# Router logits by column quarters, gate bias by a 128-row selector, and routed bookkeeping one block ahead, in a graph-attention and expert kernel

## The chip, the cores and the metric

The kernel runs on one core of a Trainium2 chip. The metric is the device time of one execution in microseconds (us), from the first to the last instruction with what lies around it. The engines are TensorE (PE in the profile, with PEld for its weight loads), VectorE (DVE), ScalarE (ACT), GpSimd (POOL) and SyncE (SP), which issues most of the DMAs. Each engine runs its instructions in order, and they wait for each other through semaphores.

## The reference

There are 16 batches of 512 tokens with 256 features, in float32. What is computed, cut to its core:

```python
h = layernorm(x)
q, k, v = h @ Wq.T, h @ Wk.T, h @ Wv.T            # 8 heads of 32
c = softmax(where(adj, q k / sqrt(32), -inf)) @ v
gate = sigmoid(concat([c, h]) @ Wg.T + bg)
x = x + gate * h + (1 - gate) * c
f = layernorm(x)                                   # 8192 tokens
w, idx = top_k(softmax(f @ router_w), 2)           # 8 experts, 2 each
x = x + sum_k w_k * (silu(f @ Wg[e]) * (f @ Wu[e])) @ Wd[e] + (silu(f @ Sg) * (f @ Su)) @ Sd
```

## The kernel before

The kernel has two phases with a barrier between them.

**Attention phase.** Its loop goes over batches, in software-pipelined passes. Each pass has 32 positions, here called slots: one slot for each tile of 128 queries of one head. In a slot TensorE makes a score matmul (L439, 96 rows by 512 keys), and the four transposes of an older slot's probabilities (L449). VectorE adds the mask and takes the maximum (L792), ScalarE takes the exponential (L568) and copies the transposed probabilities to SBUF (`pt`, L556). Every eighth slot, TensorE multiplies the probabilities with V (L470), in four column quarters: the weights are 32 columns wide, and each head's result lands in 32 of the 128 partitions.

The other work of a batch is cut into units, and the table `UNIT_AT` gives each a slot. L is the router's logits of two batches back, Q, K and V are the projections, C the transposes of the attention's result, R the ranks of tokens in their expert, Z the gate for a quarter of the tokens, P and X are transposes of the normalised inputs. A unit writes one of three PSUM banks, and another engine copies it out; TensorE waits until the unit three before has been copied (`g_free`). So a pass runs in this order: L0 in slots 0 and 1, Q1 in 2 and 3, K1 in 4 and 5, V0 and V1 in 6 to 9, C0, C1, R0 in 10 to 12, Z0 to Z3 in 14 to 17, P0, P1 in 18 and 19, Q0, K0 in 22 to 25, X0, X1 in 29 and 30.

Matmuls whose operands are split in a high and a low float32r part come in threes (L354 to L356). L0 is in plain float32 (L412): for each of four token tiles and two halves of the features, 128 columns of `z` are the weights, and the 8 columns of `router_w` stream. The profile shows each such matmul as two records. Z begins with the bias (L397): a matmul with 2 rows of ones and the 2 rows of `bg2`, the high and the low part of the bias, 256 columns wide.

ScalarE copies the logits to `lg` (L516), and `choose` on VectorE takes the two best from there, in slot 3.

**Expert phase.** After 16 shared blocks come 39 routed blocks of 512 or 256 tokens, each with the weights of one expert. For each block n, TensorE makes gate and up products for parts 0 and 1, turns (transposes, L1261) the tokens `xb` of block n+1, makes the down product of block n-1 and then parts 2 and 3. VectorE casts and splits the weights of block n+1 (L1392, L1407), and makes `take(n)` between the product of part 2 and that of part 3: it reads from `xb` the token numbers (`ix`) and weights (`wt`) of the block, which ScalarE and GpSimd use for the scaled copy (L1348) and the scatter-add (L1155). `xb`, `ix` and `wt` each have two buffers. SyncE, in one queue, loads the weights (`raw`) and then `xb` of block n+1; the buffer of `xb` is free when block n-1 has been turned and taken:

```python
if not before:
    sp.wait_ge(s_tk, (n - SH) * TK)
load_routed(n + 1, 1 - s)
```

Of the kernel before, what the change touches and what calls it, by code (L numbers as in the profile page):

```python
# [5 lines left out]
P = 128  # L6
# [15 lines left out]

UNIT_AT = {"L0": 0, "Q1": 2, "K1": 4, "V0": 6, "V1": 8, "C0": 10, "C1": 11, "R0": 12, "Z0": 14, "Z1": 15, "Z2": 16,
           "Z3": 17, "P0": 18, "P1": 19, "Q0": 22, "K0": 24, "X0": 29, "X1": 30}
HALVES = "LQKV"

# [8 lines left out]
def attention_phase(nc, sems, x, adj, wqkv, wgate, bg, router_w, xn_dram, x1_dram, xt2_dram, xg_dram,  # L35
# [20 lines left out]
    RING = 8  # L56
# [6 lines left out]
    with ctx:  # L63
# [44 lines left out]
        bg2 = sb("bg2", [P, D], F32R)  # L108
        ones2 = sb("ones2", [P, P], F32R)
        rw = sb("rw", [P, KF, E])  # L110
        ident_b = sb("ident_b", [P, P], BF16)
        below = sb("below", [P, P], BF16)
# [62 lines left out]
        s_lo = sem("s_lo")  # L175
        s_half = sem("s_half")


# [40 lines left out]
        def has(b, name, att, pre, post):  # L219

            kind = name[0]
            return (late(b) if kind in "RL" else att if kind == "V" or name in ("Q1", "K1") else
                    post if kind in "CZX" else pre)
# [8 lines left out]

        def bank(par, name):
            return G[ORDER.index(name) % 3]

# [113 lines left out]
        def _(pe):  # L349
# [13 lines left out]
            def do_unit(b, par, name, piece, end):  # L363
                B, A = b + 1, b - 1
                o = bank(par, name)
                k = int(name[1])
# [25 lines left out]
                elif name[0] == "Z":  # L392
                    if isinstance(b, int) and b == 1:
                        pe.wait_ge(s_set, 7)
                    pe.wait_ge(g_free, unit(b, "C1") + 1)
                    tok = slice(P * k, P * k + P)
                    pe.matmul(o[:, 0:D], ones2[0:2, :], bg2[0:2, :], start=True, stop=False)  # L397
                    for kf in range(KF):
                        split(o[:, 0:D], xt_h[s][:, kf, tok], xt_l[s][:, kf, tok],
                              wg_h[:, KF + kf, :], wg_l[:, KF + kf, :], False, False)  # L400
                    for kf in range(KF):
                        last = split(o[:, 0:D], ct_h[:, kf, tok], ct_l[:, kf, tok],
                                     wg_h[:, kf, :], wg_l[:, kf, :], False, kf == KF - 1)
                elif name[0] == "X":
                    pe.wait_ge(s_xn2, A * NT + NT)
                    last = turn(o, xn2, k)
                elif name[0] == "L":
                    pe.wait_ge(g_free, unit(b - 1, "X1") + 1)
                    zt = z[:, :, :].rearrange("p i d -> p (i d)")
                    for i in (2 * piece, 2 * piece + 1):  # L410
                        for kf in range(KF):
                            last = pe.matmul(o[:, E * i:E * i + E], zt[:, N * kf + P * i:N * kf + P * i + P],  # L412
                                             rw[:, kf, :], start=kf == 0, stop=kf == KF - 1)
                elif name[0] == "R":

# [70 lines left out]
        def _(act):  # L486
# [4 lines left out]
            def evacuate(b, par, name):  # L491
                B, A = b + 1, b - 1
                o = bank(par, name)
                k = int(name[1])
                act.wait_ge(g_full, unit(b, name) + 1)
                if name[0] in "ZL":
                    act.wait_ge(g_free, unit(b, name))
# [13 lines left out]
                elif name[0] == "C":  # L511

                    act.activation(ct_h[:, k, :], o[:, :], ACT.Copy).then_inc(g_hi, 1)
                elif name[0] == "L":
                    act.wait_ge(s_rt, (b - 2) * RT)
                    act.activation(lg[:, :, :], o[:, 0:NT * E].rearrange("p (i e) -> p i e", e=E),  # L516
                                   ACT.Copy).then_inc(g_free, 1)
# [70 lines left out]
        def _(dve):  # L588
            zf = z[:, :, :].rearrange("p i d -> p (i d)")
            df = diff[:, :, :].rearrange("p i d -> p (i d)")  # L590

            dve.memset(f32(ones2[:, :]), 1.0).then_inc(s_set, 1)

# [6 lines left out]
            def prepare():  # L600
# [8 lines left out]

                dve.tensor_copy(bgh[:, :], bgt[:, :]).then_inc(s_set, 1)  # L610
                dve.wait_ge(s_set, 5)
                dve.tensor_tensor(wg_l[:, :, :], x1[:, :, :], f32(wg_h[:, :, :]), ALU.subtract).then_inc(s_lo, 1)
# [3 lines left out]
                dve.wait_ge(s_lo, 5)  # L616
                dve.wait_ge(s_rt0, 4)
                dve.nop().then_inc(s_set, 2)

# [20 lines left out]
            def low(b, par, name):  # L640

                B, A = b + 1, b - 1
                o = bank(par, name)
                k = int(name[1])
# [67 lines left out]
            def choose(A):  # L712

                rt = A * RT
                dve.wait_ge(g_free, unit(A + 2, "L0") + 1)
                dve.wait_ge(s_rt, rt)
# [209 lines left out]
def ffn_phase(nc, sems, w_dram, xt2_dram, x1_dram, xg_dram, out, ident, msum, xn2, idx, s_scat, nb, region,  # L926
# [50 lines left out]
    with ctx:  # L977
# [73 lines left out]
        wb = sb("wb", [P, NT])  # L1051
        wt = [sb(f"wt{s}", [P, NT]) for s in range(2)]
        ix = [sb(f"ix{s}", [P, NT], U32) for s in range(2)]

# [56 lines left out]
        def _(pool):  # L1111
# [29 lines left out]
            def add(n, s, first):  # L1141
# [12 lines left out]
                for i in range(tiles(n)):  # L1154
                    pool.indirect_dma_start(  # L1155
                        out=out, out_offset=bass.IndirectOffsetOnAxis(ap=ix[s][:, i:i + 1], axis=0),
                        in_=yb[s][:, i, :], in_offset=None, compute_op=ALU.add).then_inc(s_acc, 16)
# [165 lines left out]
        def _(act):  # L1323
# [13 lines left out]
            def out_(n, s, first):  # L1337
# [6 lines left out]
                for j in range(2):  # L1344
                    act.wait_ge(y_full, n * 2 + j + 1)
                    for ii in range(tiles(n) // 2):
                        i = tiles(n) // 2 * j + ii
                        last = act.activation(yb[s][:, i, :], OB[j][:, D * ii:D * ii + D], ACT.Copy,  # L1348
                                              scale=wt[s][:, i:i + 1])
                    last.then_inc(s_y[j], 1)  # L1350
# [27 lines left out]
        def _(dve):  # L1378
# [60 lines left out]
            def take(n, s):  # L1439
# [4 lines left out]
                dve.wait_ge(s_xb[s], (n - s) * 8 + 16)  # L1444
                if n >= SH + 2:
                    dve.wait_ge(s_acc, acc(r - 1))
                if n > SH:
                    dve.wait_ge(s_tk, t0)
                dve.nop().then_inc(s_held_dve, 1)
                dve.tensor_copy(own[:, :], (hef if is_half(r) else tef)[:, c:c + 1]).then_inc(s_tk, 1)  # L1450
                dve.tensor_copy(ix[s][:, 0:tl], xb[s][:, 0:tl, WT]).then_inc(s_tk, 1)
                dve.wait_ge(s_tk, t0 + 2)
# [4 lines left out]
                dve.wait_ge(s_tk, t0 + 4)  # L1457
                dve.tensor_tensor(wt[s][:, 0:tl], wa[:, 0:tl], wb[:, 0:tl], ALU.add).then_inc(s_tk, 1)

# [113 lines left out]
            def body(n, s, shared, before, after):  # L1573
# [13 lines left out]
                if after is not None:  # L1587
                    low_x(n + 1, 1 - s, after)
                if after is False:
                    high_routed(n + 1, 1 - s, 2)  # L1590
                    low_routed(n + 1, 1 - s, 2)
                if before:
                    out_shared(n - 1, 1 - s)
                mul(n, s, 2)
                if not shared:
                    take(n, s)
                mul(n, s, 3)
# [76 lines left out]
```

## Time and profile before

| | before |
|---|---|
| median of 3 runs | 1965.34 us (1961.91 to 1969.79) |
| the profiled execution | 1960.68 us, of which the span is 1959.0 us |
| busy: TensorE, VectorE, ScalarE, GpSimd | 91%, 66%, 56%, 34% of the span |
| mean granted TensorE clock | 0.973 of full speed |
| score matmuls (attention phase) | 27.1 to 947.1 us |
| turns of routed blocks | 1269.3 to 1918.5 us |

Times inside the profile are counted from the first instruction. A matmul's duration overlaps with its neighbours', so what counts is the time from one start to the next. A clock of 1.00 stands for 2.4 GHz, one of 0.50 for 1.2 GHz.

### The profile page before, as it was taken

To read this page: it belongs to the slowest core of one execution; us is meant where nothing else is said; L and a number is where in the kernel's file an instruction comes from. 1 tells how busy PE (TensorE), PEld (TensorE's weight loads), DVE (VectorE), ACT (ScalarE), POOL (GpSimd) and SP (SyncE) were. 2 spreads that over 40 slices of the span, in tenths; PEclk is the share of its full clock that TensorE was granted. 3 is DMA by queue.
4 is the path that set the end of the run, shared out by engine and by line. 5 is a ranking of instruction groups with operands and counts; after the bars stand their busy time and mean duration, and the time that the engine had idled before them with its cause. 6 is when DMAs were issued, how large, how long until landed. Compare 5 with 4: busy or idle time off the path is not lost. (4 is left out here: it accounts for less than half of the span.)

```text
span 1959.0 us, 36000 instructions
## 1 busy us (share of the span) xinstructions
PE 1791.2 (91%) x12597; PEld 1502.0 (77%) x12597; DVE 1293.2 (66%) x3149; ACT 1098.3 (56%) x2489; POOL 667.4 (34%) x515
## 2 busy tenths in 40 slices
PE   5899999999999999999649999999999999999997
PEld 4677777777777777777538888888888888888886
DVE  5567767667767767766545444467777776777773
ACT  4887777788778887777413333333333434334342
POOL 1035443345444335533446000003343433333334
PEclk8999999999999999999869999999999999999998
DMA  5444555454455444454235322336555555555653
GB/s 146 115 130 120 156 162 141 143 152 125 144 162 157 140 147 132 134 167 115 82 119 184 104 89 88 129 141 157 157 144 163 128 163 137 159 152 157 154 157 44
DMA packets 141330, 269.20 MB, mean 137 GB/s; under 512 B 15456, under 2 KB 92640, under 8 KB 136160
## 3 DMA queue, kind: packets, MB, share of 16 engines
q1 hardware_dynamic: 112608, 226.19, 37.2%
q0 software_dynamic: 28128, 39.93, 10.5%
q8 instruction: 103, 1.69, 0.4%
q10 hardware_dynamic: 416, 0.79, 0.2%
q14 instruction: 75, 0.61, 0.1%
HBM read 141.99 MB, written 74.52 MB: 111 GB/s over the span
## 5 line engine op out<-in xcount | busy, mean ns | idle before, releaser
L792 DVE CUSTOM_DVE_ANT_0 pf<-bank,bias_q 128x512 f32<-128x512 f32 x512 | 350.6, 687 | 268.5 <-PE bank L439 258.9
L1155 POOL DMA_INDIRECT out_x<-yb,ix x142 | 235.9, 1662 | 640.0 <-ACT yb L1348 554.6
L568 ACT ACTIVATE pf<-pf,nmax 128x512 f32<-128x512 f32 x512 | 373.6, 730 | 47.4 <-DVE nmax L792 46.1
L1360 ACT ACTIVATE ah<-am 128x512 fp32r<-128x512 f32 (+1 forms) x220 | 133.1, 605 | 432.2 <-DVE am L1423 432.2
L1266 PE MATMUL fbank<-xh,wh 128*128 128x512 f32 (+1 forms) x880 | 335.8, 382 | 13.1 <-DVE xl L1413 13.1
L1267 PE MATMUL fbank<-xl,wh 128*128 128x512 f32 (+1 forms) x880 | 335.7, 381 | 0.0
L1268 PE MATMUL fbank<-xh,wl 128*128 128x512 f32 (+1 forms) x880 | 335.4, 381 | 0.0
L449 PE MATMUL bank<-ident,pf 128*128 128x128 f32 x2048 | 314.6, 276 | 17.9 <-ACT pt L556 17.7
L556 ACT ACTIVATE pt<-bank 128x512 f32<-128x512 f32 x512 | 307.5, 601 | 14.1 <-PE bank L449 13.7
L449 PEld LDWEIGHTS bank<-ident,pf 128*128 128x128 f32 x2048 | 256.2, 142 | 73.7 <-issue 23.4
L439 PE MATMUL bank<-stack 96*128 96x512 f32 x512 | 235.3, 460 | 37.2 <-DVE nmax L792 25.9
L1426 DVE TENSOR_TENSOR al<-am,ah 128x512 fp32r<-128x512 f32 (+1 forms) x220 | 144.9, 659 | 147.7 <-ACT ah L1360 147.7
L1266 PE MATMUL fbank<-wh,ah 128*128 128x256 f32 x824 | 237.3, 288 | 2.1 <-issue 2.1
L1268 PE MATMUL fbank<-wh,al 128*128 128x256 f32 x824 | 234.1, 284 | 0.0
L1267 PE MATMUL fbank<-wl,ah 128*128 128x256 f32 x824 | 233.7, 284 | 0.0
L1266 PEld LDWEIGHTS fbank<-xh,wh 128*128 128x128 f32 x880 | 166.4, 189 | 45.6 <-DVE xl L1413 13.6
L1423 DVE TENSOR_TENSOR am<-sg,fbank 128x512 f32<-128x512 f32 (+1 forms) x220 | 143.1, 650 | 87.7 <-PE fbank L1268 87.4
L1268 PEld LDWEIGHTS fbank<-xh,wl 128*128 128x128 f32 x880 | 166.4, 189 | 34.0
L1267 PEld LDWEIGHTS fbank<-xl,wh 128*128 128x128 f32 x880 | 166.4, 189 | 32.1
L1358 ACT ACTIVATE sg<-fbank 128x512 f32<-128x512 f32 (+1 forms) x220 | 124.5, 566 | 101.2 <-PE fbank L1268 97.4
L1266 PEld LDWEIGHTS fbank<-wh,ah 128*128 128x128 f32 x824 | 157.2, 191 | 2.9 <-issue 2.3
L439 PEld LDWEIGHTS bank<-stack 96*128 96x128 f32 x512 | 98.8, 193 | 78.8 <-DVE nmax L792 31.6
(208 smaller groups left out, 3229.4 us busy)
## 6 DMA issues: line engine op xcount, KB each, us to landing
raw<-in_w_all SPq DMA_DIRECT2D x39, 1536.0 KB, 8.4
stack<-qk SPq DMA_DIRECT2D x378, 128.0 KB, 2.4
xb<-xg_dram SPq DMA_DIRECT2D x32, 520.0 KB, 3.9
adj_i<-in_adj SPq DMA_DIRECT2D x32, 512.0 KB, 5.4
xn<-in_x SPq DMA_DIRECT2D x16, 512.0 KB, 5.3
xn_dram<-xn SPq DMA_DIRECT2D x16, 512.0 KB
xp<-in_x SPq DMA_DIRECT2D x16, 512.0 KB, 6.3
xnp<-xn_dram SPq DMA_DIRECT2D x16, 512.0 KB, 7.3
```

The source lines that it names most:

```text
L439: pe.matmul(S[p % 2][:, :], stack[0:SR, hd, 0, P * tq:P * tq + P], stack[0:SR, hd, 1, :], start=True, stop=True).then_inc(s_full, 1)
L449: last = pe.transpose(T[ep % 2][:, P * kt:P * kt + P], pf[ep % RING][:, P * kt:P * kt + P], ident[:, :])
L556: act.activation(pt[r][:, j, :, P * (tq % 2):P * (tq % 2) + P], T[ep % 2][:, :].rearrange("p (k q) -> p k q", q=P), ACT.Copy).then_inc(t_f ...
L568: act.activation(pf[i][:, :], pf[i][:, :], ACT.Exp, bias=nmax[:, i:i + 1], scale=-1.0, accum_out=den[:, g, tq, j:j + 1]).then_inc(p_exp, 1)
L792: dve.tensor_tensor_reduce(pf[r][:, :], S[p % 2][:, :], bias_q[1 - par][:, tq, :], -SCALE, -3.0 * MASKED, ALU.add, ALU.min, nmax[:, r:r + ...
L1155: pool.indirect_dma_start(out=out, out_offset=bass.IndirectOffsetOnAxis(ap=ix[s][:, i:i + 1], axis=0), in_=yb[s][:, i, :], in_offset=None, ...
L1266: pe.matmul(out_, lh, rh, start=first, stop=False)
L1267: pe.matmul(out_, lh, rl, start=False, stop=False)
L1268: return pe.matmul(out_, ll, rh, start=False, stop=last)
L1360: act.activation(ah[s][:, m, 0:cols], am[m % 2][:, 0:cols], ACT.Copy).then_inc(s_ah, 1)
L1423: dve.tensor_tensor(am[m % 2][:, 0:cols], sg[m % 2][:, 0:cols], UB[m % 2][:, 0:cols], ALU.mult).then_inc(s_am, 1)
L1426: dve.tensor_tensor(al[s][:, m, 0:cols], am[m % 2][:, 0:cols], f32(ah[s][:, m, 0:cols]), ALU.subtract).then_inc(s_al, 1)
```

## The change

It has three parts.

1. **Logits.** L0 takes one slot instead of two. The weights are now `router_w`, padded with zeros to 32 columns (`rw_wide`), and 128 tokens of `z` stream; the four token tiles write the four column quarters of the bank. ScalarE copies the 128x128 result to `lgt`. A new unit M0 in slot 1 transposes it in one go, and ScalarE copies 8 of each 32 columns to `lg` in slot 2. A pass now has 19 units, so the bank follows the unit's running number.
2. **Gate bias.** `ones2[0:2]` gives way to `pick2`, a 128-row matrix with ones in rows 0 and 1 and zeros elsewhere.
3. **Routed blocks.** `take(n + 1)` runs in the body of block n, behind the split of the turned tokens and ahead of the cast of the third part of the weights. `wt` and `ix` have four buffers instead of two.

```diff
-UNIT_AT = {"L0": 0, "Q1": 2, "K1": 4, "V0": 6, "V1": 8, "C0": 10, "C1": 11, "R0": 12, "Z0": 14, "Z1": 15, "Z2": 16,
+UNIT_AT = {"L0": 0, "M0": 1, "Q1": 2, "K1": 4, "V0": 6, "V1": 8, "C0": 10, "C1": 11, "R0": 12, "Z0": 14, "Z1": 15, "Z2": 16,
-HALVES = "LQKV"
+HALVES = "QKV"
...
-        def bank(par, name):
-            return G[ORDER.index(name) % 3]
+        def bank(b, name):
+            return G[unit(b, name) % 3]
...
-                    pe.matmul(o[:, 0:D], ones2[0:2, :], bg2[0:2, :], start=True, stop=False)
+                    pe.matmul(o[:, 0:D], pick2[:, :], bg2[:, :], start=True, stop=False)
...
                 elif name[0] == "L":
                     pe.wait_ge(g_free, unit(b - 1, "X1") + 1)
-                    for i in (2 * piece, 2 * piece + 1):
-                        for kf in range(KF):
-                            last = pe.matmul(o[:, E * i:E * i + E], zt[:, N * kf + P * i:N * kf + P * i + P],
-                                             rw[:, kf, :], start=kf == 0, stop=kf == KF - 1)
+                    for kf in range(KF):
+                        for i in range(NT):
+                            last = pe.matmul(o[DK * i:DK * i + DK, 0:P], rw_wide[:, kf, :],
+                                             zt[:, N * kf + P * i:N * kf + P * i + P], start=kf == 0, stop=kf == KF - 1)
+                elif name[0] == "M":
+                    pe.wait_ge(g_free, unit(b, "L0") + 1)
+                    last = pe.transpose(o[:, 0:P], lgt[:, :], ident[:, :])
...
                 elif name[0] == "L":
+                    act.wait_ge(g_full, unit(b - 1, "M0") + 1)
+                    act.activation(lgt[:, :], o[:, 0:P], ACT.Copy).then_inc(g_free, 1)
+                elif name[0] == "M":
                     act.wait_ge(s_rt, (b - 2) * RT)
-                    act.activation(lg[:, :, :], o[:, 0:NT * E].rearrange("p (i e) -> p i e", e=E),
+                    act.activation(lg[:, :, :], o[:, 0:P].rearrange("p (i c) -> p i c", c=DK)[:, :, 0:E],
                                    ACT.Copy).then_inc(g_free, 1)
...
-            dve.memset(f32(ones2[:, :]), 1.0).then_inc(s_set, 1)
+            dve.memset(f32(pick2[:, :]), 0.0).then_inc(s_pick, 1)
+            dve.wait_ge(s_pick, 1)
+            dve.memset(f32(pick2[0:2, :]), 1.0).then_inc(s_set, 1)
+            dve.memset(rw_wide[:, :, :], 0.0).then_inc(s_pick, 1)
...
+                dve.tensor_copy(rw_wide[:, :, 0:E], rw[:, :, :]).then_inc(s_pick, 1)
...
             def choose(A):
-                dve.wait_ge(g_free, unit(A + 2, "L0") + 1)
+                dve.wait_ge(g_free, unit(A + 2, "M0") + 1)
...
-        wt = [sb(f"wt{s}", [P, NT]) for s in range(2)]
-        ix = [sb(f"ix{s}", [P, NT], U32) for s in range(2)]
+        RING = 4
+        wt = [sb(f"wt{i}", [P, NT]) for i in range(RING)]
+        ix = [sb(f"ix{i}", [P, NT], U32) for i in range(RING)]
...
             def take(n, s):
-                if n >= SH + 2:
-                    dve.wait_ge(s_acc, acc(r - 1))
+                if n >= SH + RING:
+                    dve.wait_ge(s_acc, acc(r - RING + 1))
...
                 if after is False:
+                    take(n + 1, 1 - s)
+                if after is False:
                     high_routed(n + 1, 1 - s, 2)
                     low_routed(n + 1, 1 - s, 2)
                 if before:
                     out_shared(n - 1, 1 - s)
                 mul(n, s, 2)
-                if not shared:
-                    take(n, s)
                 mul(n, s, 3)
```

## Rows read from the trace of the kernel before

**Rows 1.** Waits of TensorE, 1320 to 1935 us: total, times, longest.

```profile
PE fbank L1261 <- DMA xb<-xg_dram: 17.1, 13, 2.1
```

**Rows 2.** Stretches (slots 8-12, 15-18): length; busy PE, PEld, DVE, ACT, POOL; clock; DMA.

```profile
558.00:567.77 9.77, 8.28 (x67) 7.42 (x65) 9.06 (x30) 7.62 (x19) 5.29 (x3) 1.00 0.48 114
...
574.50:585.00 10.50, 10.50 (x77) 9.20 (x76) 4.06 (x12) 6.90 (x18) 7.75 (x8) 1.00 0.55 186
```

**Rows 3.** Instructions in order, TensorE, slot 15: start, duration.

```profile
574.80 0.40 PE L439 MATMUL bank<-stack 96*128 96x512 f32 x1
...
575.56 0.38 PE L397 MATMUL bank<-bg,ones 2*128 2x256 f32 x1
575.88 0.39 PE L354 MATMUL bank<-wg_h,xt_h 128*128 128x256 f32 x1
576.10 0.28 PE L355 MATMUL bank<-wg_l,xt_h 128*128 128x256 f32 x1
...
577.41 0.40 PE L439 MATMUL bank<-stack 96*128 96x512 f32 x1
```

**Rows 4.** The same, a slot of unit V.

```profile
560.87 0.40 PE L439 MATMUL bank<-stack 96*128 96x512 f32 x1
...
562.25 0.40 PE L439 MATMUL bank<-stack 96*128 96x512 f32 x1
```

**Rows 5.** The same, PV in slot 28.

```profile
541.22 1.93 PE L470 MATMUL bank<-pt,v 128*32 128x256 f32 x32
543.08 0.50 PE L439 MATMUL bank<-stack 96*128 96x512 f32 x1
```

**Rows 6.** The same, slots 31, 0 and 1, with idle time and releaser.

```profile
545.32 0.49 PE L439 MATMUL bank<-stack 96*128 96x512 f32 x1
...
546.00 0.48 PE L439 MATMUL bank<-stack 96*128 96x512 f32 x1
...
547.56 1.03 PE L412 MATMUL bank<-rw,z 128*128 128x8 f32 x8 [0.64 <-DVE z L667]
548.45 0.48 PE L439 MATMUL bank<-stack 96*128 96x512 f32 x1
...
550.01 0.48 PE L439 MATMUL bank<-stack 96*128 96x512 f32 x1
```

**Rows 7.** Instructions in order, ScalarE, slots 1 and 2.

```profile
547.62 0.59 ACT L556 ACTIVATE pt<-bank 128x512 f32<-128x512 f32 x1
...
550.20 0.20 ACT L516 ACTIVATE lg<-bank 128x32 f32<-128x32 f32 x1 [1.26 <-PE bank L412]
```

**Rows 8.** Instructions in order, VectorE, one routed block.

```profile
1421.45 0.70 DVE L1392 CAST wh<-raw 128x1024 fp32r<-128x1024 f32 x1 [1.15 <-PE fbank L1268]
...
1426.81 0.16 DVE L1458 TENSOR_TENSOR wt<-wa,wb 128x4 f32<-128x4 f32 x1
```

**Rows 9.** Instructions in order, SyncE, two loads of `xb`.

```profile
1427.83 0.34 SPq L1192 DMA_DIRECT2D xb<-xg_dram  x1
...
1445.54 0.34 SPq L1192 DMA_DIRECT2D xb<-xg_dram  x1
```

**Rows 10.** Instructions in order, TensorE, a turn after a wait.

```profile
1397.91 0.40 PE L1268 MATMUL fbank<-xh,wl 128*128 128x512 f32 x1
...
1400.51 0.37 PE L1266 MATMUL fbank<-wh,ah 128*128 128x256 f32 x1
```

**Rows 11.** The same, a turn without a wait.

```profile
1414.38 0.39 PE L1268 MATMUL fbank<-xh,wl 128*128 128x512 f32 x1
...
1415.40 0.36 PE L1266 MATMUL fbank<-wh,ah 128*128 128x256 f32 x1
```

**Rows 12.** Busy us by stretch, at the lower clock (columns as in rows 2).

```profile
313.30:320.10 6.80, 6.80 (x24) 5.63 (x24) 2.72 (x19) 3.22 (x9) 0.00 (x0) 0.50 0.98 327
...
839.00:842.40 3.40, 3.40 (x13) 2.73 (x13) 0.70 (x2) 2.68 (x7) 0.00 (x0) 0.50 0.89 253
```

**Rows 13.** Instructions in order, TensorE, before that stretch.

```profile
838.30 1.11 PE L412 MATMUL bank<-rw,z 128*128 128x8 f32 x8
```

More of the change, by code:

```diff
@@ L108, in attention_phase @@
         bg2 = sb("bg2", [P, D], F32R)
-        ones2 = sb("ones2", [P, P], F32R)
+        pick2 = sb("pick2", [P, P], F32R)
         rw = sb("rw", [P, KF, E])
+        rw_wide = sb("rw_wide", [P, KF, DK])
+        lgt = sb("lgt", [P, P])
         ident_b = sb("ident_b", [P, P], BF16)
@@ L176, in attention_phase @@
         s_half = sem("s_half")
+        s_pick = sem("s_pick")
         s_held_pe, s_held_dve, s_held_pool, s_held_sp = (sem(f"s_held_{e}") for e in ("pe", "dve", "pool", "sp"))
@@ L221, in has @@
             kind = name[0]
-            return (late(b) if kind in "RL" else att if kind == "V" or name in ("Q1", "K1") else
+            return (late(b) if kind in "RLM" else att if kind == "V" or name in ("Q1", "K1") else
                     post if kind in "CZX" else pre)
@@ L364, in do_unit @@
                 B, A = b + 1, b - 1
-                o = bank(par, name)
+                o = bank(b, name)
                 k = int(name[1])
@@ L492, in evacuate @@
                 B, A = b + 1, b - 1
-                o = bank(par, name)
+                o = bank(b, name)
                 k = int(name[1])
                 act.wait_ge(g_full, unit(b, name) + 1)
-                if name[0] in "ZL":
+                if name[0] in "ZLM":
                     act.wait_ge(g_free, unit(b, name))
@@ L610, in prepare @@
                 dve.tensor_copy(bgh[:, :], bgt[:, :]).then_inc(s_set, 1)
+                dve.wait_ge(s_pick, 2)
+                dve.tensor_copy(rw_wide[:, :, 0:E], rw[:, :, :]).then_inc(s_pick, 1)
                 dve.wait_ge(s_set, 5)
@@ L617, in prepare @@
                 dve.wait_ge(s_rt0, 4)
+                dve.wait_ge(s_pick, 3)
                 dve.nop().then_inc(s_set, 2)
@@ L642, in low @@
                 B, A = b + 1, b - 1
-                o = bank(par, name)
+                o = bank(b, name)
                 k = int(name[1])
@@ L1155, in add @@
                     pool.indirect_dma_start(
-                        out=out, out_offset=bass.IndirectOffsetOnAxis(ap=ix[s][:, i:i + 1], axis=0),
+                        out=out, out_offset=bass.IndirectOffsetOnAxis(ap=ix[n % RING][:, i:i + 1], axis=0),
                         in_=yb[s][:, i, :], in_offset=None, compute_op=ALU.add).then_inc(s_acc, 16)
@@ L1348, in out_ @@
                         last = act.activation(yb[s][:, i, :], OB[j][:, D * ii:D * ii + D], ACT.Copy,
-                                              scale=wt[s][:, i:i + 1])
+                                              scale=wt[n % RING][:, i:i + 1])
                     last.then_inc(s_y[j], 1)
@@ L1450, in take @@
                 dve.tensor_copy(own[:, :], (hef if is_half(r) else tef)[:, c:c + 1]).then_inc(s_tk, 1)
-                dve.tensor_copy(ix[s][:, 0:tl], xb[s][:, 0:tl, WT]).then_inc(s_tk, 1)
+                dve.tensor_copy(ix[n % RING][:, 0:tl], xb[s][:, 0:tl, WT]).then_inc(s_tk, 1)
                 dve.wait_ge(s_tk, t0 + 2)
@@ L1457, in take @@
                 dve.wait_ge(s_tk, t0 + 4)
-                dve.tensor_tensor(wt[s][:, 0:tl], wa[:, 0:tl], wb[:, 0:tl], ALU.add).then_inc(s_tk, 1)
+                dve.tensor_tensor(wt[n % RING][:, 0:tl], wa[:, 0:tl], wb[:, 0:tl], ALU.add).then_inc(s_tk, 1)
             def count_blocks():
```

## The prediction

> **What bounds the kernel now.** I read the page first, then the waits of TensorE in the routed blocks, then stretches of the attention, and last the order of instructions in one slot of each kind. TensorE is the busiest engine of the page by far. In the routed blocks TensorE has one wait alone: the turn of the next block (L1261) waits for the DMA of `xb`, 13 times, 17.1 us [rows 1]. So these blocks are bound by TensorE and by that load. In attention TensorE is busy in all of the gate's slots, 10.50 of 10.50 us, while VectorE has 4.06 and ScalarE 6.90; in the stretch of slots 8 to 12 VectorE sets the pace with 9.06 of 9.77 [rows 2]. A saving in a TensorE-bound slot should move all later slots: the other two wait there, and VectorE's slow stretch begins after one in which it idles, so it shifts with the rest.
>
> **Gate bias by 128 rows.** Nothing is added on TensorE: `ones2[0:2]`, two rows, becomes `pick2`, 128 rows, with the same 256 columns. Slot 15 takes 577.41 - 574.80 = 2.61 us from its score matmul to the next, with 13 matmuls of 256 columns [rows 3]. A slot of V has the same score and transposes and six such matmuls, 562.25 - 560.87 = 1.38 us [rows 4]. The last eleven steps of slot 15 take 577.41 - 576.10 = 1.31 us, 0.12 each. Thirteen such matmuls should give 1.38 + 7 x 0.118 = 2.21 us. The missing 0.40 lies about the 2-row matmul, which alone takes 575.88 - 575.56 = 0.32 us to the next. PV (L470) is the other place where the array leaves the 128*128 form; there too the last of its matmuls is followed by a long step: 32 records from 541.22 to 543.08 are 1.86 us, some 0.05 each and 0.3 at the end [rows 5]. So I take the 0.40 for the change of form, gone with 128 rows. Z0 waits for `ct_l`, which hides the entry; it saves the exit, 0.32 - 0.12 = 0.20. A pass saves 3 x 0.40 + 0.20 = 1.40, and sixteen passes **22.4** (bounds: 0 if the form is not the cause, 25.6 if Z0 saves all).
>
> **Logits.** The first piece of old L0 takes 548.45 - 547.56 = 0.89 us for eight records. Slot 1, with the second, takes 550.01 - 548.45 = 1.56; slot 31, which has no unit, 546.00 - 545.32 = 0.68 [rows 6]. New slot 1 is slot 31 and one transpose, 0.79, so it saves 0.77. New slot 0 holds all eight f32 matmuls, 16 records as before, in four column quarters. No row has 128 columns in this form. At PV's step they take 0.78 + 0.31 = 1.09 us, at half of it 0.71; the entry hides in the wait for `z`, 0.64 us [rows 5, 6]. I take 0.91, as in the old piece, and 0.75 saved in all (bounds 0.57 and 0.95). The added wait: M0 stands on TensorE behind ScalarE's copy of L0, and behind M0 stand Q1 and every later slot. L0 ends near 548.3. No row has a 128x128 copy: 0.20 us for 128x32 and 0.59 for 128x512 are its ends [rows 7]; I take 0.28 by size. `lgt` is there at 548.7, and until 549.1 TensorE has a score and four transposes, so no stall, with 0.4 to spare. ScalarE meets the new copy ahead of the `pt` copy that now starts at 547.62, and so holds it until 548.6; the transposes that need its bank come at 549.4, and the 1.26 us that ScalarE idles before the old `lg` copy pay for it [rows 7]. If that cover fails, 0.6 us a batch are lost. The new `lg` copy keeps its place in slot 2, so `choose` in VectorE's slot 3 is not later. Fourteen batches have both L0 and attention: 14 x 0.75 = **10.5** (bounds: 0, and 13). The two passes behind them are a chain where one more copy meets one piece less: nothing. The setup's two memsets and one copy on VectorE are under 1 us. The banks now turn by unit number, and the wait is still for the unit three before.
>
> **Take ahead.** SyncE issues `xb` of block n+1 only after take(n-1), which stands behind the third product of block n-1. It ends at 1426.97, and the load goes at 1427.83 [rows 8, 9]; TensorE needs it some 9 us later in full blocks and sooner about a half block. The 13 waits are 17.1 us [rows 1]. A turn that waited also restarts slowly: 1397.91 to 1400.51 is 2.60 us, and an unhindered one, 1414.38 to 1415.40, is 1.02 [rows 10, 11]. That is 1.58 more, where the mean wait is 17.1 / 13 = 1.32; so 0.26 more each, 3.4 in all. After the change take(n-1) runs one body earlier, so the load is issued a block, 17.7 us, sooner [rows 9]. It then lies in SyncE's queue behind the weights of the same block, which were themselves held back behind the old take and go some 4 us earlier. Both together land within a block today, and have nearly two then. On VectorE the take, 0.8 us, now stands ahead of the cast of part 2, which idles 1.15 us for TensorE anyway [rows 8]: it costs nothing there. Without that cover it delays the third product by 0.8, and the bank that this frees is due only in the next block. The ring of four eases the wait for the scatter-adds. The first three routed turns keep their waits, as their loads stand behind the stores of shared blocks. **Sum 17.1 + 3.4 = 20.5** (bounds 17 and 23).
>
> **Clock.** In attention the granted clock was 0.50, that is 1.2 GHz, in five stretches, one of 6.8 and four of 3.4 us, the first and the last of them shown [rows 12]. The last came at 839.0, in the second group of old L0's 8-column matmuls, which begins at 838.30 [rows 13]; before the first group TensorE idles for `z`, 0.64 us in the batch of [rows 6]. TensorE was busy all through the 20.4 us, so up to 10.2 are lost; I take 9.5, as other engines pace a part. The new slots are shorter and go on into Q1's 512-column matmuls sooner, so I expect the falls to vanish (bounds: 0, or 14 lost with a fall in each of the other nine batches).
>
> **The sum.** 22.4 + 10.5 + 20.5 + 9.5 = 62.9. The profiled execution took 1960.7 (span 1959.0), 4.7 under the median of 1965.3. That gives 1897.8 by the profile, 1903 by the median.
>
> **Rivals.** (a) All as summed: 0.55, 1903; its own range 1895 to 1911. (b) The clock falls stay, because the wait for `z` and the transposes about it stay: 0.20, 1912. (c) The logits bring nothing, because the quarter records cost as PV's or M0 waits: 0.10, 1913. (d) VectorE or ScalarE becomes the bound in the shortened slots: 0.07; half of the 42.4 us of attention are lost, 1924. Against it, VectorE is idle for 6.4 of 10.5 us of the gate's slots and ScalarE for 3.6 [rows 2]. (e) `xb` still comes late, now behind its weights in one queue: 0.04, 1923. (f) Slower than before: new L0 and M0, with a wait between them, keep the clock at 1.2 GHz. A stretch of 3.4 us costs 1.6; to undo the other 53 us and add 10 takes 39 stretches more than now, three in each batch: 0.02, 1975. The rest, 0.02, is no change.
>
> The Trainium skill has a rule against the logits part. Its page TensorEngine Tiling (Array Packing), Instruction Overhead, says that a matmul of one column lasts as long as one of sixty, with about 60 cycles of overhead. By that figure the old sixteen records would be an estimated 0.4 us a batch and the change a loss of some 8 us there, 1922. The trace does not agree: the old records step at 0.11 us [rows 6]. This is one more road to (c), and I give it no chance of its own.
>
> **Range and chances.** 1890 to 1925 holds (a) to (e) and the bounds of the unsure terms. About 0.5%, 10 us, is what a measurement of this kernel can tell from no change. Faster 0.95, same 0.03, slower 0.02.
>
> **What would show it.** Slots 15 to 17 at 2.2 us with L397 stepping at 0.12; slots 0 and 1 at 3.25 together; no idle before M0; no wait at a turn after the third routed one; granted clock 1.00 through the attention. The prediction is wrong if the gate's slots stay at 2.6, or if the batches get no shorter while VectorE's waits for TensorE shrink.

## The result, and the profile after

The changed kernel takes 1902.32 us, the median of 4 runs (1898.95 to 1906.11); the kernel before, run beside it, 1965.84. The ratio is 0.9677, with a 95% interval of 0.965 to 0.9705: 3.2% faster, 63.5 us by the medians. The forecast was 1903, with 62.9 us saved. The profiled execution took 1903.38 us (span 1901.7), 57.3 less than the profiled one of before. In the groups of the experiments below, the ratios leave out one slow run of the kernel before (2551.93 us, granted clock 0.646), which counts only in the median 2076.47.

TensorE's gate slot 15 in the order of instructions, as in [rows 3] (start, duration):

```profile
553.17 0.48 PE L445 MATMUL bank<-stack 96*128 96x512 f32 x1
...
554.64 0.36 PE L400 MATMUL bank<-bg,pick 128*128 128x256 f32 x1 [0.55 <-DVE ct_l L671]
554.84 0.28 PE L357 MATMUL bank<-wg_h,xt_h 128*128 128x256 f32 x1
...
556.25 0.40 PE L445 MATMUL bank<-stack 96*128 96x512 f32 x1
556.49 0.60 PE L455 MATMUL bank<-ident,pf 128*128 128x128 f32 x4
556.84 0.36 PE L400 MATMUL bank<-bg,pick 128*128 128x256 f32 x1
557.05 0.28 PE L357 MATMUL bank<-wg_h,xt_h 128*128 128x256 f32 x1
557.16 0.28 PE L358 MATMUL bank<-wg_l,xt_h 128*128 128x256 f32 x1
...
558.46 0.40 PE L445 MATMUL bank<-stack 96*128 96x512 f32 x1
```

Slot 15 is 558.46 - 556.25 = 2.21 us, where it was 2.61, and slot 14 is 556.25 - 553.17 = 3.08, with its wait for `ct_l` still in it. From the bias matmul to the next is 0.21 us now, 0.32 before.

Slots 0 and 1 of the same batch, as in [rows 6]:

```profile
528.67 0.48 PE L445 MATMUL bank<-stack 96*128 96x512 f32 x1
...
530.24 0.65 PE L415 MATMUL bank<-z,rw_wide 128*32 128x128 f32 x16 [0.64 <-DVE z L682]
530.81 0.50 PE L445 MATMUL bank<-stack 96*128 96x512 f32 x1
531.15 0.60 PE L455 MATMUL bank<-ident,pf 128*128 128x128 f32 x4
531.59 0.27 PE L419 MATMUL bank<-ident,lgt 128*128 128x128 f32 x1
531.62 0.48 PE L445 MATMUL bank<-stack 96*128 96x512 f32 x1
```

All sixteen logit records take 530.81 - 530.24 = 0.57 us. Slots 0 and 1 are 531.62 - 528.67 = 2.95 us together; before they were 550.01 - 546.00 = 4.01 [rows 6]. M0 (L419) shows no idle time in front of it, in this batch or any other. But this is a batch that went well. In another, slot 1 looks so (one line of ScalarE among TensorE's):

```profile
473.34 0.50 PE L445 MATMUL bank<-stack 96*128 96x512 f32 x1
473.47 0.28 ACT L522 ACTIVATE lgt<-bank 128x128 f32<-128x128 f32 x1 [0.54 <-PE bank L415]
...
474.12 0.27 PE L419 MATMUL bank<-ident,lgt 128*128 128x128 f32 x1
...
475.09 0.50 PE L445 MATMUL bank<-stack 96*128 96x512 f32 x1 [0.70 <-DMA stack<-qk]
```

The next head's first score waits 0.70 us for its part of `stack`. That wait was there in few batches before. In the waits of TensorE over the fourteen batches from the first score of batch 1 to that of batch 15, first before (79.9 to 894.2 us), then after (78.5 to 862.8):

```profile
PE bank L439 <- DMA stack<-qk: 1.5, 3, 1.0
```

```profile
PE bank L445 <- DMA stack<-qk: 7.2, 14, 1.1
```

Every other wait of TensorE's matmuls in these two stretches agrees within 0.2 us (for VectorE's `nmax` 20.9 in both), apart from one of 0.4 that is new, so this is the one that the change brought. It comes with the logits: on one chip, TensorE's wait for `stack` in these fourteen batches is 4.6 us in logits only and 1.8 in take only. All twelve transfers of `stack` leave SyncE's queue in a row:

```profile
800.96 8.51 SPq L269 DMA_DIRECT2D stack<-qk  x12
```

The stretch itself by the view of stretches (length; busy PE, PEld, DVE, ACT, POOL; granted clock; DMA), before and after:

```profile
79.90:894.20 814.30, 752.86 (x6273) 600.56 (x6271) 577.71 (x1778) 642.83 (x1569) 335.84 (x272) 0.99 0.50 144
```

```profile
78.50:862.80 784.30, 716.72 (x6286) 572.84 (x6284) 578.40 (x1778) 643.47 (x1582) 341.00 (x272) 1.00 0.52 150
```

VectorE and ScalarE are busy as long as before, TensorE 36 us less, and 30 of them shorten the stretch. The clock was low in two stretches of 3.4 us here (five, 20.5 us, before), neither of them at L0:

```profile
213.20:216.60 3.40, 3.40 (x43) 2.17 (x45) 2.58 (x7) 3.27 (x9) 3.19 (x4) 0.51 0.58 134
493.10:496.50 3.40, 3.40 (x39) 2.27 (x42) 2.73 (x7) 3.40 (x9) 3.19 (x4) 0.51 0.64 149
```

In the routed blocks, the wait of [rows 1] has gone from the waits of TensorE; what is left of it in the whole span is the first three routed turns, of which two, and the first without a wait, stand here:

```profile
PE fbank L1277 <- DMA xb<-xg_dram: 7.3, 3, 2.8
```

```profile
1231.87 1.09 PE L1277 MATMUL fbank<-ident,xb 128*128 128x128 f32 x8 [1.66 <-DMA xb<-xg_dram]
1252.63 1.09 PE L1277 MATMUL fbank<-ident,xb 128*128 128x128 f32 x8 [2.81 <-DMA xb<-xg_dram]
...
1292.69 1.03 PE L1277 MATMUL fbank<-ident,xb 128*128 128x128 f32 x8
```

By the starts of turns in the two traces, the 57.3 us come from four parts: 31.4 up to the first score of batch 15 (894.2 to 862.8), 6.0 from there to the first routed turn (1269.3 to 1231.9), -0.9 in the first three turns, and 20.8 from the fourth turn to the last (588.9 to 568.1). Of the 31.4, 30.0 lie in the fourteen batches. Summed there by slot, slots 14 to 17 (the gate) are 19.3 us shorter, slots 0 and 1 11.4, slots 2 to 4 2.2, slot 12 is 2.9 longer, and every other slot agrees within 0.1.

### The profile page after: what moved, and what is told of

Its sections match the earlier page's. It is cut to its first block and busy times, and to the rows that moved or that the text cites. A ratio compares the mean times of both kernels' runs of the same rounds, so it can differ in the third digit from the quotient of the medians.

```text
span 1901.7 us, 36088 instructions
## 1 busy us (share of the span) xinstructions
PE 1739.3 (91%) x12613; PEld 1463.7 (77%) x12613; DVE 1293.3 (68%) x3152; ACT 1096.8 (58%) x2505; POOL 685.5 (36%) x515
## 5 line engine op out<-in xcount | busy, mean ns | idle before, releaser
L1171 POOL DMA_INDIRECT out_x<-yb,ix x142 | 249.1, 1754 | 607.3 <-ACT yb L1364 521.3
```

Source lines behind the costliest of these rows:

```text
L1171: pool.indirect_dma_start(out=out, out_offset=bass.IndirectOffsetOnAxis(ap=ix[n % RING][:, i:i + 1], axis=0), in_=yb[s][:, i, :], in_offse ...
```

## The experiments

Every kernel ran beside the kernel before, on the same chip. That took 2072.66 us beside bias only, logits only, take only and early loads; 2076.47 beside bias only again, both, 64 rows and one quadrant at a time; 1963.36 beside the changed kernel again, late scatters and 96 rows; and 1966.43 beside bias only for the third time. So ratios are compared, and times only within one of these four groups. There is one trace of the kernel before, from another group than these.

**The parts alone.** Bias only: `pick2` and its matmul, nothing else.

```
-                    pe.matmul(o[:, 0:D], ones2[0:2, :], bg2[0:2, :], start=True, stop=False)
+                    pe.matmul(o[:, 0:D], pick2[:, :], bg2[:, :], start=True, stop=False)
```

> The kernel before with only the 128-row bias matmul. If the 2-row form itself is the cause and a TensorE-bound slot passes its saving on, slots 15 to 17 take 2.21 us, slot 14 loses 0.20, a batch 1.40, and the time falls by 22.4, to 1943 (1938 to 1949, the clock's falls left to chance). If VectorE or ScalarE takes the saving up elsewhere in the batch, the slots are short but the time stays above 1955.

Measured: 2062.62, ratio 0.9948 (0.992 to 0.9977), which is 10.8 us by the ratio and 10.0 by the medians; less than half of the 22.4.

Logits only: quadrants, L0, `lgt`, M0, and the banks by unit number.

```
-HALVES = "LQKV"
+HALVES = "QKV"
...
+                    for kf in range(KF):
+                        for i in range(NT):
+                            last = pe.matmul(o[DK * i:DK * i + DK, 0:P], rw_wide[:, kf, :],
```

> The kernel before with only L0 in column quarters and M0. Slots 0 and 1 together 2.94 us at best instead of 4.01, which is 15 us in fourteen batches. If the DMAs of the stacked heads then come late for slots 1 to 3, as in the changed kernel (17 waits, 17.2 us, against 5 and 11.3), 6 of it are lost. If the clock's falls belong to old L0's slots they vanish and give 9.5: 1947. If they fall elsewhere as often, nothing: 1957. Forecast 1950, as a mean of these two.

Measured: 2045.02, ratio 0.987 (0.9829 to 0.9911), 27.6 us by the medians, where the forecast of this run had 15. TensorE's mean granted clock was 0.953, against 0.943 and 0.942 in the other two parts. At half speed below the rest, 0.01 of 2044 us is some 41 us fewer at the low clock; a stretch of 3.4 us costs 1.6 (batches of the kernel before are 59.07 us long with one and 57.50 without), so the clock is worth an estimated 19 of the 27.6 us here, and the logits themselves 8. The 1.6 us come from another chip, and some of the stretches that are gone lay in the stalls shown below, where they cost less. Against the trace of take only, whose attention is that of the kernel before, the fourteen batches are 24.6 us shorter: 12.2 in slots 0 and 1, 9.2 in slots 2 to 4, where ten low stretches of 3.4 us have gone, and 5.0 in slots 19 and 20; slot 12 is 1.4 longer.

Take ahead only: the order in the body, and the ring of four.

```
+                    take(n + 1, 1 - s)
...
-                if not shared:
-                    take(n, s)
```

> The kernel before with only the bookkeeping one block ahead and the ring of four. The 13 waits of the later turns vanish, 20.5 us: 1945 (1942 to 1949). The first three turns waited 5.3 us before and 7.3 in the changed kernel. If that growth comes from the take, which now stands ahead of the shared blocks' additions and so of the stores and loads behind them, it is seen here too; if it comes from the phase of the DMAs, it is not.

Measured: 2051.93, ratio 0.9905 (0.9869 to 0.994), 20.7 us by the medians, where the sum has 20.5. In TensorE's waits, three for `xb` are left, as in the changed kernel; in bias only there are 16, of which the first three take 5.8 us. So the waits of the first three turns scatter about 6 us with and without this part, and a growth by the take is not shown:

```profile
PE fbank L1262 <- DMA xb<-xg_dram: 6.3, 3, 2.7
```

**Why the bias gave half.** In the trace of bias only the gate's slots are 2.21 us long, as forecast. But a little later, in slot 19, TensorE, ScalarE and VectorE stand still while GpSimd's scatters go on (instructions in order, all engines):

```profile
617.39 0.48 PE L440 MATMUL bank<-stack 96*128 96x512 f32 x1
618.13 0.96 POOL L883 DMA_INDIRECT xg_dram<-xn,idx  x1 [0.30 <-issue]
619.40 0.96 POOL L883 DMA_INDIRECT xg_dram<-xn,idx  x1 [0.30 <-issue]
620.27 0.38 ACT L511 ACTIVATE z<-bank 128x256 f32<-128x256 f32 x1 [3.49 <-remote]
620.49 0.69 DVE L795 CUSTOM_DVE_ANT_0 pf<-bank,bias_q 128x512 f32<-128x512 f32 x1 [4.37 <-remote]
...
622.88 0.77 PE L440 MATMUL bank<-stack 96*128 96x512 f32 x1
```

Slot 19 takes 622.88 - 617.39 = 5.49 us there; with the same code on another chip, below, it takes 1.1. "Remote" is what the profile names where it finds no event of the core that released the engine. The stall shows in nearly all passes of the kernels of the first two groups. In most of them VectorE starts again 15.2 us after slot 14's start, in take only (gate slots of 2.60) as in bias only (2.21); so on those chips most of what the gate's slots save is waited out. Summed over the fourteen batches, slots 14 to 17 of bias only are 18.9 us shorter than those of take only, and slots 18 to 21 are 12.6 us longer. I ran bias only again, twice.

> The bias matmul over 128 rows alone, a second time. Theory: slots 14 to 17 shorten by 0.2, 0.4, 0.4 and 0.4 us in each of 16 passes, 22.4 us, and this reaches the end only where nothing later in the loop waits for something else: in the first run of this kernel all engines stood still in slot 19 until 15.2 us after slot 14's start, and 1.2 of the 1.4 us of a pass were given back there (10.8 us came out). Where slot 19 has no such stall, 22 us of the kernel before's time go (ratio 0.989); where it has, about 11 (0.995). Rival: half of the gain is lost to a lower clock, then the stall makes no difference, and the low-clock stretches are longer than before by about 10 us.

Measured: 2061.86, ratio 0.9929 (0.9905 to 0.9954), 14.6 us by the medians; the stall is there, and in the trace, again against take only's, slots 18 to 21 give back 17.2 of 18.8 us. But this ratio lies between the 0.989 and the 0.995 of the theory, so the size of the loss isn't settled by it.

> The bias matmul over 128 rows alone, once more. Two runs gave 10.8 and 14.7 us, both with a stall of all engines in slot 19 of each pass that ended 15.2 us after slot 14's start whatever the gate slots took. Theory, that the stall swallows the rest: if this run shows no such stall, the whole 22.4 us of the forecast's sum come out, ratio 0.987 to 0.990. Rival, that the freed time goes to a lower clock or to another wait in the loop anyway: 11 to 15 us, 0.993 or more, without a stall too. If the stall is there, 0.992 to 0.995, and the question stays with the traces.

Measured: 1948.79, ratio 0.9914 (0.989 to 0.9937), 17.6 us by the medians, and no stall. The gain lies between the 0.987 to 0.990 that I had expected and the rival's 0.993: each of the two may have a part. The shortest length of each slot in batches 2 to 14, summed over a batch and below called its floor, fell from 57.34 to 55.98 us, by 1.36, where the forecast had 1.40; sixteen times that is 21.8. Against it, nine stretches at the low clock stand in the fourteen batches, 34.1 us in all, where the kernel before had 20.5. Seven of the nine began in slot 1 or 2, in old L0's second part or right behind it:

```profile
825.81 0.81 PE L413 MATMUL bank<-rw,z 128*128 128x8 f32 x6
826.48 0.48 PE L440 MATMUL bank<-stack 96*128 96x512 f32 x1
...
827.34 0.78 PE L355 MATMUL bank<-xt_h,wqkv_h 128*128 128x512 f32 x1
```

```profile
827.00:830.40 3.40, 3.40 (x13) 2.88 (x12) 1.49 (x7) 2.23 (x6) 0.00 (x0) 0.50 0.89 280
```

Here the first view is TensorE's order, the second that stretch. The 13.6 us more at the low clock cost an estimated 13.6 x 1.6 / 3.4 = 6.4, and 21.8 - 6.4 = 15.4 is within the interval (12.4 to 21.6 us of 1966.43). But this compares single executions. By the mean granted clocks of all runs on this chip (0.968 in six, 0.9695 in eleven of the kernel before) bias only has some 5 us more at the low clock, with a standard error of 4, so the clock's part is between nothing and about 6 us and is not shown more closely.

**What the 0.40 us of a gate slot were.** The bias matmul over 64 and over 96 rows in place of 128; the rows left out hold zeros.

```
-                    pe.matmul(o[:, 0:D], pick2[:, :], bg2[:, :], start=True, stop=False)
+                    pe.matmul(o[:, 0:D], pick2[0:64, :], bg2[0:64, :], start=True, stop=False)
```

> The changed kernel with the bias matmul over 64 rows (the rows left out hold zeros). Theory, that what was paid for is leaving and entering a form of less than 128 rows: slots 15 to 17 take 2.6 us again, as with 2 rows. Rival, that two rows are slow as such: they stay at 2.2.

> The changed kernel with the bias matmul over 96 rows. With 64 rows slots 15 to 17 took 2.6 us, with 128 they take 2.2. If any number of rows other than 128 is a form of its own: 2.6 again. If more than 64 rows count as the full form: 2.2.

Measured, in slot 15 of either trace, first 64 rows, then 96:

```profile
597.65 0.60 PE L455 MATMUL bank<-ident,pf 128*128 128x128 f32 x4
598.18 0.38 PE L400 MATMUL bank<-bg,pick 64*128 64x256 f32 x1
598.50 0.38 PE L357 MATMUL bank<-wg_h,xt_h 128*128 128x256 f32 x1
```

```profile
551.31 0.60 PE L455 MATMUL bank<-ident,pf 128*128 128x128 f32 x4
551.66 0.36 PE L400 MATMUL bank<-bg,pick 96*128 96x256 f32 x1
551.87 0.28 PE L357 MATMUL bank<-wg_h,xt_h 128*128 128x256 f32 x1
```

With 64 rows the slot is 2.59 us, as with 2; with 96 it is 2.21, as with 128. The bias starts 0.53 us after the transposes do with 64 rows and 0.35 with 96 (0.18 to enter the form), and the step behind it is 0.32 against 0.21 (0.11); the next step, 0.22 against 0.11, has another 0.11. So it isn't the number of rows as such but a change of form: 64 rows pay as 2 do, and 96 rows, like the score matmuls' own 96, count as the full form. The Trainium skill, TensorEngine Tiling (Array Packing), Key Properties, says that a change of tiling mode drains TensorE; its list of modes (Available Configurations) has rows of 128, 64 and 32. The trace agrees that a change costs time, 0.4 us for a change and back; what the engine does in it no row shows. The single run of 96 rows took 1896.77, inside the spread of the changed kernel on that chip (1894.53 to 1909.96), and its fourteen batches had no stretch at the low clock. On a chip with the stall, the 64 rows, a single run too, took 2019.11, and one quadrant at a time, with gate slots 0.38 us shorter, 2019.82: nothing of these slots shows in the time there.

**What the logits' quadrants cost.** One quadrant after another in place of one chunk after another.

```
-                    for kf in range(KF):
-                        for i in range(NT):
+                    for i in range(NT):
+                        for kf in range(KF):
```

> The changed kernel with the router's logits one column quadrant after another (the four matmuls of a quadrant in a row) in place of one chunk after another. Theory, that the 16 records take 0.57 us since neighbours lie in different quadrants and overlap: they take 0.9 us or more, as my estimate of 0.91 had it. Rival, that a matmul of 32 columns is short as such: 0.57 to 0.6 us in either order.

Measured:

```profile
572.79 0.67 PE L415 MATMUL bank<-z,rw_wide 128*32 128x128 f32 x16 [0.64 <-DVE z L682]
573.39 0.50 PE L445 MATMUL bank<-stack 96*128 96x512 f32 x1
```

0.60 us: it makes hardly a difference whether neighbours lie in one quadrant or in different ones. The rival holds for the order. Why the old records were slow shows in the groups of weight loads (count | busy us, mean ns), first of before, then of the changed kernel:

```profile
L412 PEld LDWEIGHTS bank<-rw,z 128*128 128x128 f32 x256 | 33.4, 204 | 14.4 <-DVE z L667 14.4
```

```profile
L415 PEld LDWEIGHTS bank<-z,rw_wide 128*32 128x32 f32 x256 | 6.7, 112 | 14.4 <-DVE z L682 14.4
```

Before, `z` was the weight, 128 columns a record, for eight columns of moving data, and the weight loads ran without a gap; now the weight is `rw_wide`, 32 columns. The mean step from one record to the next fell from 0.11 to 0.57 / 16 = 0.036 us. By the Trainium skill, TensorE: Matmul & The Clock Gate, LDWEIGHTS (loading the stationary operand), a load's time goes by its columns, whatever the rows. The trace goes the same way, with 204 and 112 ns here, and with 183 and 191 for the bias weights of 2 and of 128 rows, but a quarter of the columns is not a quarter of the time.

What sets the new pace is another thing. Cut at later records, the views of the new logits and of PV [rows 5] are these (a row's start is that of its first record, xN counts the records left; first two of the changed kernel, then two of before):

```profile
530.35 0.54 PE L415 MATMUL bank<-z,rw_wide 128*32 128x128 f32 x12
530.46 0.43 PE L415 MATMUL bank<-z,rw_wide 128*32 128x128 f32 x8
```

```profile
541.46 1.69 PE L470 MATMUL bank<-pt,v 128*32 128x256 f32 x28
541.67 1.48 PE L470 MATMUL bank<-pt,v 128*32 128x256 f32 x24
```

Both go in groups of four records, 0.11 us apart with 128 moving columns and 0.22 with 256. The weights are the same 32 columns in both, so in this form the step went by the moving columns and not by the weight load.

**The waits that are left.** Early loads: the changed kernel, with the loads of the second and third routed block issued ahead of the stores of the block before.

```
+                if n == SH - 1:
+                    loads(n + 1, 1 - s, False, True, False)
+                if n == SH:
+                    loads(n + 1, 1 - s, False, False, False)
```

> The changed kernel, with the loads of the second and third routed blocks ahead of the stores of the last shared ones in SyncE's queue. If those turns wait because their loads stand behind the stores, their waits (5.6 of 7.3 us), slow restarts and the clock's fall behind the third go: 8 us, 1894. If the DMA engines are the bound there, with 4 MB for two blocks in 20 us, the waits only move: 1900 to 1902.

Measured: 2004.16, ratio 0.968 (0.9644 to 0.9716). One wait for `xb` is left, and the first and fourth turns lie 53.23 us apart; in take only they lie 1441.19 - 1379.49 = 61.70 apart, and 60.82 in the changed kernel. So the theory holds for the waits, and some 8 us go there, but the ratio is no better than that of the changed kernel:

```profile
PE fbank L1285 <- DMA xb<-xg_dram: 1.0, 1, 1.0
```

```profile
1340.46 1.09 PE L1285 MATMUL fbank<-ident,xb 128*128 128x128 f32 x8 [1.05 <-DMA xb<-xg_dram]
...
1393.69 1.04 PE L1285 MATMUL fbank<-ident,xb 128*128 128x128 f32 x8
```

Both: early loads, and head 3's three transfers of `stack` from GpSimd at slot 29.

```
-                    refs(B, unit(b, "K0") + 1, range(0, GRP, 2) if first(b) else range(GRP))
+                    refs(B, unit(b, "K0") + 1, range(0, GRP, 2) if first(b) else range(GRP - 1))
...
+                    if p == HEAD_AT and pre and not first(b):
+                        send_head(pool, GRP - 1, s_ref3p)
```

> The changed kernel, with two waits taken out that it left or made: the second and third routed blocks are loaded ahead of the stores of the block before (the first three turns' waits, 7.3 us), and the three stack transfers of head 3 go out of GpSimd's queue at slot 29 in place of SyncE's (the scores' waits for stacks, 17.2 us after against 11.3 before). Theory: the rows of both waits fall below 3 us and 12 below the first row of stacks, and the time is 10 to 14 us under the changed kernel's, ratio 0.960 to 0.962. Rival: the wait for the stacks hides behind another (the scores' bank, the exponential of the head before), then only the loads' 7 us come out, 0.965; and if GpSimd is late at slot 29, slot 3 or the scatters slip and it is 0.968 or more.

Measured: 2007.62, ratio 0.9674 (0.9648 to 0.97), the same as early loads and not the 0.960 to 0.962 of the theory. The wait for the stacks did not shrink: 19.9 us, 23 times, in the whole span, where early loads has 14.3 and 13. In the changed kernel most of it is head 3's, in slot 3 (8 of 14 waits in the fourteen batches); here 13 of 20 are head 2's, in slot 2, 5 head 1's and 2 head 0's (batch 8, TensorE):

```profile
509.58 0.80 PE L450 MATMUL bank<-stack 96*128 96x512 f32 x1 [1.08 <-DMA stack<-qk]
```

So relieving the last head of the queue only moved the wait to the heads before: SyncE's nine issues still take 5.92 us, and all begin when K0's low part is done. Neither version is shown to beat the changed kernel, which wasn't run in those two groups; by the ratios the three are level. But the ratios of different chips don't settle it: one quadrant at a time, which is the changed kernel but for 0.03 us a batch, took 2019.82 in its single run, 12 us more than both beside it.

**All parts together, again, and the scatters later.** The changed kernel beside one that holds GpSimd's scatters back.

```
                     pool.wait_ge(s_rt, A * RT + RT_IDX)
+                    pool.wait_ge(g_full, unit(A + 2, "Z3") + 1)
```

> The changed kernel beside its parts on the same chip. Alone the parts brought 10.8 to 14.7 us (bias), 27.6 (logits) and 20.7 (take). Theory, that each removes time of its own: their sum, 59 to 63 us, ratio 0.970 to 0.972. Rival, that the parts take each other's gain (the wait for the stacks, the stall in slot 19): 50 us or less, 0.976 or more.

> The changed kernel with GpSimd's eight scatters of a pass held back until TensorE has done the last gate piece (slot 17), some 4.5 us later than they start now. Where a pass shows the stall of all engines in slot 19: if the scatters make it, it moves with them and ends 1.6 us after the last of them, some 19.8 us after slot 14's start; or it goes. If it comes of something else at this place of the program (its code being loaded), it stays in slot 19 and ends as before or sooner. The time falls only if it goes, then by up to 40 us; if it moves, it stays within 10 us.

Measured: the changed kernel 1903.73, ratio 0.9679 (0.9636 to 0.9723), 59.6 us by the medians and 63.0 by the ratio. The parts alone make 58.3 by the medians (10.0 + 27.6 + 20.7) and 57.4 by the ratios. So the rival, 50 us or less, did not come. But contrary to what the expectation says, the parts ran on another chip, and the agreement is in part chance: there the stall took from the bias and the clock gave to the logits. With late scatters 1910.57, ratio 0.9727 (0.9692 to 0.9761): no gain. The scatters began 7 us later, not 4.5. This trace has no stall in slot 19, so what makes it could not be told from this run, and stays open; there is no time of a version with fewer scatters. One thing in the eight traces with the stall bears on it: the first of the fourteen batches has no scatters yet in its pass, and its slot 19 takes 1.1 us in all eight. That speaks for the scatters but doesn't show it, since a first pass differs in more than this.

## Why the prediction was right

**Gate bias** (22.4): right in mechanism and size. 2.61 to 2.21 us in slots 15 to 17 and 0.20 in slot 14 are the forecast's figures, the floor of a batch fell by 1.36 in bias only against 1.40, and the fourteen batches lose 19.3 us in the gate's slots, where 14 x 1.40 is 19.6. 64 and 96 rows show that the form is the cause. Two details were wrong. The prediction calls PV the other place where the array leaves the 128*128 form, but every score matmul is 96*128 [rows 3]; that this costs nothing only the run of 96 rows showed. And the bias matmul steps at 0.21 us, not at the 0.12 that was to be a sign; the rest of the 0.40 lies before it and in the step behind it. Alone, the edit brought 17.6 us where there is no stall; the clock may have taken a part back there. In the whole change old L0, where most of those falls came, is gone.

**Logits** (10.5): the parts missed on both sides. The sixteen records were costed at 0.91 us and take 0.57, below the lowest figure of the prediction, 0.71. That figure took half of PV's steps but all of its 0.31 us at the end. By the single records PV's last group of four takes 0.33 us to the next score, 0.22 of it the group's own step; the logits' last group takes 0.25, and three steps of 0.11 ahead of it make the 0.57. Slots 0 and 1 shorten by 1.06 us, not 0.75, some 15 us over fourteen batches. The copy of `lgt` (0.28) and M0 without idle are as forecast. Against this stands a wait that no rival of mine named: with slots 0 and 1 shorter, the first scores of heads 1 to 3 come sooner than their transfers. It grew by 7.2 - 1.5 = 5.7 us in TensorE's matmul rows. The batch's floor fell by 57.34 - 54.93 = 2.41, 33.7 us in fourteen; 30.0 came out, although the low clock gave some 6.5 more. So about 10 us went in slots 1 to 3, and the weight loads, which start sooner, name them: they waited for the stacks for 13.8 us against 2.8. What is left of the logits is some 5 us, where the sum had 10.5 and rival (c) nothing.

**Clock** (9.5): right in kind, too large. The sign, 1.00 through the attention, did not come in full. At the slots of L0 no fall is left in the profiled execution of the change; its two begin in slot 12, behind an idle time of 0.9 us and ahead of the 8-column matmuls of the router's ranks. The saving is an estimated (20.5 - 6.8) x 1.6 / 3.4 = 6.4 us, and slot 12 is 2.9 us longer for the two. The executions of 96 rows (none) and of the changed kernel again (three stretches, 10.2 us) show how far it scatters.

**Take ahead** (20.5): right in the main. 20.8 us lie between the fourth and the last routed turn, and take only brought 20.7. Of the 20.8, 17.1 are the waits; the other 3.7 were forecast as slow restarts (3.4), but the kernel before also has a low stretch of 3.4 us there, at 1381.7, right behind a turn that waited, and the changed kernel has none, so how much is restart and how much clock is not told apart. The first three turns kept their waits, as said, and all three grew, from 5.3 to 7.3 us.

**The sum.** 62.9 forecast, 57.3 in the profiled executions, 63.5 by the medians. In the trace: 22 bias, 5 logits, 6 clock and 20 take ahead make 53; the other 4 us lie outside the fourteen batches. Some 3 of them may be clock: between the start and the routed blocks, outside those batches, the low stretches that differ are 6.8 us at 57.3 and 3.4 each at 951.6 and 961.8 before, and 3.4 each at 59.6 and 926.6 after. That is an estimate by the same price. The profiled execution of before was 4.7 under its median, that of after 1.1 over, so the hit within 1 us is partly luck; by the trace the forecast was 6 us too hopeful, mostly in logits and clock. Rivals (d) and (e) did not come: VectorE's waits for TensorE shrank with the slots, from 219 to 189 us in the fourteen batches, and no routed turn from the fourth on waits.

## What to carry to other kernels

Look at both sides of any matmul with few rows in a stream of full ones: here 2 and 64 rows cost 0.4 us more than 96 or 128 filled up with zeros. Where the moving data is narrow, try the narrower operand as the weight: here 8 moving columns against 128 of weights took 0.11 us a record, the other way round a mean of 0.036. Before you shorten slots that run ahead of a queue of transfers, list what the following matmuls wait for and how much slack each has; the shortest slack is your next wait, and here moving only the last transfer to another queue moved the wait to the heads before.

## What the runs showed of the hardware that was not expected

In two of the four groups TensorE, ScalarE and VectorE stood still once in nearly every pass of the same loop: mostly 5 to 7 us for a slot that takes 1.1 elsewhere, the kernel before 2073 to 2076 us against 1963 to 1966. The stall mostly ended 1.5 to 1.7 us after the last of eight scatters; that it comes of them is not shown, since the run with late scatters had no stall to move. It takes gains away that are real in the trace (12.6 of 18.9 us of the gate's slots in bias only), so a part timed alone there doesn't give its worth elsewhere.

Where the low clock falls changed with the slots, and scattered. The kernel before had five stretches in fourteen batches, all of them beginning in slot 1 or 2, at or just behind old L0; with shorter gate slots alone there were nine, seven of them there and two in slot 12; with the new logits none was left there, and the changed kernel's two traces have two and three, all in slot 12. These are counts of single executions; by the mean clocks of all runs only the fall from before to after (0.972 to 0.978 on one chip) is clear, not the rise with the gate slots alone.

In the form of four column quarters (128*32), records came in groups of four, 0.22 us apart with 256 moving columns and 0.11 with 128; with one quadrant at a time, where the four of a group are of one quarter, it is 0.11 too.
